# One program for all eight batch elements in place of a loop of four passes over two

## The reference

```
x, cond, ctx                     # (8,256,128), (8,128), (8,1601,96)
for each of 12 sublayers s:
    h = layernorm(x) * a_s(cond) + b_s(cond)
    s = 0, 1, 6, 7:   16 heads of 64 (wide): softmax(q k' / 8) v @ wo     # 0, 6 self; 1, 7 cross; 0, 1 with rotary turns
    s = 3, 4, 9, 10:  16 heads of 8 (narrow), 3, 9 self; 4, 10 cross (9 normalises h by head)
    s = 2, 5, 8, 11:  FFN 128 -> 512 -> 128 (8 and 11 gated)
    x = x + (gate_s(cond) *) result                                      # gates in 9, 10, 11
```

## Time and profile before

| | |
|---|---|
| median of 3 runs | 7247.16 us (7244.05 to 7248.84) |
| profiled execution | 7236.4 us, its span 7234.6 us |
| TensorE busy | 6467.9 us (89%), 43,254 matmuls |
| VectorE, ScalarE, GpSimd busy | 4933.3 (68%), 3985.1 (55%), 2705.2 us (37%) |
| mean granted clock of TensorE | 0.953 of full speed |
| DMA | 206 MB, mean 28 GB/s |

### The profile page before, as it was taken

One profiled execution on the slowest core, in us unless ns is written; L12 is line 12 of the kernel. 1 busy time (PEld: TensorE's weight loads), 2 busy tenths in 40 slices (PEclk: granted clock), 3 DMA queues, 4 the chain that ended last, 5 costly groups with the idle time before them and its releaser, 6 DMA issues.

```text
span 7234.6 us, 145186 instructions
## 1 busy us (share of the span) xinstructions
PE 6467.9 (89%) x43254; PEld 3723.7 (51%) x43254; DVE 4933.3 (68%) x9902; ACT 3985.1 (55%) x7106; POOL 2705.2 (37%) x2326
## 2 busy tenths in 40 slices
PE   7899989989789998998978999899897999989988
PEld 4555445644455544564445554456444555446644
DVE  6777666656677766665677776666567776766656
ACT  4455665646444566565644455655564445565556
POOL 2446115640145511564014551156401455115640
PEclk9999999999899999999989999999998999999999
DMA  3110011110111001110011110111001111011100
GB/s 80 32 26 25 23 30 28 29 29 12 45 30 30 24 21 31 30 29 26 12 46 30 30 27 19 31 28 30 26 12 46 28 27 27 19 31 28 29 19 12
DMA packets 347835, 205.96 MB, mean 28 GB/s; under 512 B 165005, under 2 KB 319981, under 8 KB 346926
## 3 DMA queue, kind: packets, MB, share of 16 engines
q1 hardware_dynamic: 347054, 196.34, 10.5%
HBM read 105.18 MB, written 1.05 MB: 15 GB/s over the span
## 4 chain that ended last, share of the span: by engine, by line
PE 65%; issue 13%; DVE 9%; ACT 8%; POOL 2%; SPq 1%; DVEq 0%; ACTq 0%; DMA 0%; POOLq 0%
PE ring L1309 32%; PE o_acc L1309 18%; PE scores L1309 14%; DVE max_part L2048 4%; ACT qop L1597 3%; ACT probs L1722 2%; POOL weight_sum L1270 1%; ACT region L1597 1%; DVE o_inv L2079 1%; DVE ring L2024 1%; ACT qm L1597 1%; DVE ring L2027 1%; DVE qop L2007 1%; PE ring L1407 1%; DVE region L2010 0%
## 5 line engine op out<-in xcount | busy, mean ns | idle before, releaser
L2048 DVE TENSOR_REDUCE max_part<-ring 128x1 f32<-128x400 f32 (+2 forms) x4608 | 2454.6, 578 | 865.6 <-PE ring L1309 849.8
L1722 ACT ACTIVATE probs<-scores 128x1024 f32<-128x1024 f32 (+1 forms) x2048 | 1915.7, 968 | 1262.8 <-PE scores L1309 895.3
L1270 POOL TENSOR_TENSOR weight_sum<-weight_sum,probs 128x512 f32<-128x512 f32 (+1 forms) x1408 | 1784.3, 1267 | 103.4 <-ACT probs L1722 4.1
L1309 PE MATMUL o_acc<-probs,region 128*32 128x256 f32 (+2 forms) x13312 | 1361.7, 389 | 0.0
L1270 POOL TENSOR_TENSOR weight_sum<-probs 128x512 f32<-128x512 f32 x256 | 324.3, 1267 | 2159.5 <-PE ring L1309 1913.6
L1597 ACT ACTIVATE region<-ring 64x400 f16<-64x400 f32 (+4 forms) x1744 | 814.4, 477 | 524.7 <-PE ring L1309 415.7
L1309 PEld LDWEIGHTS o_acc<-probs,region 128*32 128x32 f32 (+2 forms) x13312 | 590.2, 123 | 533.1 <-issue 323.3
L1597 ACT ACTIVATE qop<-ring 64x256 f16<-64x256 f32 (+1 forms) x1536 | 563.5, 374 | 485.7 <-DVE ring L2027 313.8
L1309 PE MATMUL scores<-qop,region 128*128 128x256 f16 (+1 forms) x3328 | 779.1, 275 | 18.0 <-ACT probs L1722 9.7
L1309 PE MATMUL ring<-nk,qm 128*128 128x400 f16 (+2 forms) x2560 | 718.1, 343 | 78.2 <-DVE max_part L2048 42.8
L1309 PE MATMUL scores<-qop,x_cop 128*128 128x256 f16 (+1 forms) x3328 | 775.6, 274 | 0.0
(11 more groups left out here) (160 smaller groups left out, 7583.4 us busy)
## 6 DMA issues: line engine op xcount, KB each, us to landing
x_cop<-region SPq DMA_DIRECT2D x256, 200.1 KB, 3.1
stage<-in_wide SPq DMA_DIRECT2D x512, 64.0 KB, 2.0
nk<-region SPq DMA_DIRECT2D x192, 100.1 KB, 2.2
stage<-in_wide SPq DMA_DIRECT2D x128, 128.0 KB, 2.5
v_stage<-in_wide SPq DMA_DIRECT2D x256, 64.0 KB, 1.9
wo_stage<-in_wide SPq DMA_DIRECT2D x32, 512.0 KB, 3.8
cop_few<-kop_few SPq DMA_DIRECT2D x256, 32.0 KB, 1.9
ff_w<-in_ff_w SPq DMA_DIRECT2D x24, 256.0 KB, 4.0
```

The costliest lines, as they stand in the source:

```text
L1270: pool.tensor_tensor(total, before, probs[0:rows_, g % PROBS, at:at + BANK], ALU.add)\
L1309: return pe.matmul(out, lhs, rhs, start=start, stop=stop, skip_group_check=True)
L1722: act.activation(to, src, ACT.Exp, scale=t.scale).then_inc(exp_done.sem, 1)
L2048: dve.tensor_reduce(dst, src, AX.X, ALU.max).then_inc(*release(one))
```

## The change

All four passes are one program and one plan. `make_units` runs over the pairs b, so `u` goes from 0 to 7, there are 384 units, and `Plan` orders all of them together. `sequence()` lists the preludes: (END, u - 2) stands directly ahead of (0, u). Buffers are indexed by `u % 2`, as before by u. `Count.at` returns a constant; `ago`, the credits for the first pass and the pass-end padding of the ring's counts go. The `ab` tile goes: instructions read the table `mod_flat[:, u]`. The result's store has a semaphore for each of two buffers, and VectorE waits for it two elements later; SP's wait at a pass's end goes. What is computed is the same, instruction by instruction, but for the `ab` copies.

```diff
+    for b in range(B // 2):
+        for t in ATTS:
+            for u in (2 * b, 2 * b + 1):
+                for p in range(t.units):
+                    out.append(Unit(len(out), t, u, p, chunk, wide_at, narrow_at))
...
+def sequence():
+
+    out = []
+    for b in range(B // 2):
+        for t in ATTS:
+            for u in (2 * b, 2 * b + 1):
+                if t.sub == 0 and b:
+                    out.append((END, u - 2))
+                out.append((t.sub, u))
+    return out + [(END, B - 2), (END, B - 1)]
...
@@ make_order @@
         if un.p == 0:
+            if t.sub == 0 and un.u >= 2:
+                place_prelude(END, un.u - 2, host)
             place_prelude(t.sub, un.u, host)
...
@@ Plan.pre @@
-            on("DVE", 0.4)
+
+            on("DVE", 0.4, *([("SP", ("pre", 1, u - u % 2 - 1, of_kind(1, "ctx")[-1]))] if u >= 2 else []))
...
+            sent = [("SP", ("pre", END, u - 2, m))] if s == END and u >= 2 else []
+            on("DVE", 1.3 if s == END else 0.45, pe, *sent)
...
@@ Count @@
-    def at(self, b, key, c=0):
-        return b * self.total + (self.base[key] + c + self.credit)
+    def at(self, key, c=0):
+        return self.base[key] + c + self.credit
...
@@ SP @@
-                wait((x_out_sent.sem, x_out_sent.at(b, (END, 1), 16)))
-                sp.sem_inc(x_out_free.sem, 2)
...
-            with sp.Fori(0, B // 2 - 1) as b:
-                one_pass(b, True)
-            one_pass(B // 2 - 1, False)
+            program()
...
@@ tensor, the same on the other engines @@
-            with pe.Fori(0, B // 2) as b:
-                program(b)
+            program()
...
@@ make_scores @@
-                    old, co, ago = chunk_before(g, SLOTS)
-                    pe.wait_ge(exp_done.sem, (exp_done.ago if ago else exp_done.at)(b, old.n, co + 1))
+                    if g >= SLOTS:
+                        old, co = chunk_before(g, SLOTS)
+                        pe.wait_ge(exp_done.sem, exp_done.at(old.n, co + 1))
...
@@ modulate @@
-                    dve.wait_ge(ab_ready.sem, ab_ready.at(b, (0, 0), 1))
-                    dve.tensor_scalar(h_t[:, u, :], ring[:, bank(one), 0:N], ab[:, u, 2 * sub:2 * sub + 1],
-                                      ab[:, u, 2 * sub + 1:2 * sub + 2], ALU.mult, ALU.add).then_inc(*release(one))
+                    dve.tensor_scalar(h_t[:, u % 2, :], ring[:, bank(one), 0:N], mod_flat[:, u, 2 * sub:2 * sub + 1],
+                                      mod_flat[:, u, 2 * sub + 1:2 * sub + 2], ALU.mult, ALU.add).then_inc(*release(one))
```

## The result

The changed kernel takes 7128.3 us (median of 4 runs, 7116.94 to 7131.75) against 7245.6 before (median of 4, the three of the table above and one more): ratio 0.9837, interval 0.982 to 0.9854, so 117 us less. Run again beside the experiments it stood at ratios of 0.9829 and 0.9838. The prediction was 7095, with 7000 to 7190 as its range.

The account below looks back on a forecast made before the run. The prediction took TensorE, busy 89%, as the bound wherever it has no holes. Boundaries 60 plus register steps 90 made 150 us off the profiled 7236.4, giving 7086; adjusted to the runs' median, about 7097, written 7095, range 7000 to 7190.

Parts of the forecast that it names:

- (1): Where batch pairs meet: weaving one pair's end with the next's begin saves 20 us per boundary, 60 in all (13 to 86).
- The idle-time working: At the boundary: TensorE's 41.2 us idle falls to 20.6, plus 4 from a faster clock, 25 us saved in all.
- the twin: Sublayer 4's second batch followed by sublayer 6's first, already woven inside a pass: 157.2 us, the model for the boundary.
- The other working: At the boundary: 157.2 us plus 26.0 for rotary work gives 183.2 instead of 200.6, saving 17.4 us.
- (2): Waits on TensorE, VectorE and ScalarE: removing register arithmetic ahead of them saves 90 us (0 to 258).
- TensorE's 25: TensorE's own register steps, beside its matmuls: removing them saves 25 us, lower bound nothing, 113 at 0.01 us a step.
- Rival A: Register steps on all engines are hidden, so only the boundaries pay: 7187 us; chance 0.17.
- (3): Job order moved in the first sublayer and sublayer 6 of pairs 1 to 3: costs nothing, -12 to +12 us.
- (4): Small things: the `ab` copy, its waits, the pass-end store wait and four sem_incs; costed at nothing.
- B: At the boundary, the woven end delays sublayer 0's VectorE jobs, so only the branch is saved: 7144 us; chance 0.11.
- D: At the boundary, the weave keeps the pair of stages at clock 0.67, making the kernel slower: 7275 us; chance 0.03.
- C: Boundaries and register steps both at their upper ends, 86 + 145 + 40: 6976 us; chance 0.06.

Follow-up runs that it names:

- e5: The changed kernel itself, run again unedited beside other experiments: 7113.5 us, ratio 0.9829 to the kernel before.
- e12: The changed kernel itself, run once more unedited beside other experiments: 7119.9 us, ratio 0.9838 to the kernel before.
- e1: Against the kernel before: one pair's plan written out four times in the old order, no loop, branch, register steps or weave; 7217.9 us against 7238.8, ratio 0.9968.
- e2: The changed kernel with a register step put back ahead of each wait on TensorE, VectorE and ScalarE: 7145.5 us, ratio 0.9871 to the kernel before.
- e10: The changed kernel with register steps put back ahead of the waits of VectorE and ScalarE alone: 7141.8 us, ratio 0.9866 to the kernel before.
- e9: The changed kernel with register steps put back ahead of TensorE's waits alone: 7114.3 us, ratio 0.9828 to the kernel before.
- e11: The changed kernel with TensorE's wait for a free ring bank written twice: 7140.7 us, ratio 0.9868 to the kernel before.
- e4: The changed kernel without waits its engine already made for that semaphore with the same or a higher number: 7097.3 us, ratio 0.9803 to the kernel before.

## Why the prediction was right in sum, and where its steps were not

**The sum.** 150 us were forecast, 117 came; the sign and the range held. But terms were wrong by more than the sum was, in opposite senses: that they cancelled to within 33 us is luck.

**(1) The boundary: 60 forecast, 86 to 89 found.** By the stage rows it is 29.0, 30.0 and 29.8 us for the three boundaries, a little over the upper bound of 28.8 that the sum had; some 4.3 us of each are the branch. In e5 and e12 the three come to 89 and 86. The step that failed is "I take 20, between the two workings", with the 4 us for the clock in it. The idle-time working was exact: the twin's 20.6 us of idle time was to be the woven pair's, and the pair has 20.4. What was too small is the clock: I let only the 13.9 us of the end's own matmuls speed up, but the low level had lain over others of the pair too. It lasted 34 us of the 200.6 and now 10 of the 171.6, and the pair's work went from 159.4 to 151.2, 8 us in place of 4. The other working, by the twin's length, added 26 us for rotary work, the difference of two second batches; of the first batches in the changed kernel it is 20 (75.2 against 55.0 for sublayer 6 of pair 0). The check "near 183, and not 195" came out at 171.6.

**(2) The register steps: 90 forecast, some 10 to 30 found.** e1 leaves about 9 us beside the branch, in the old order; e2 puts 24 to 30 on putting them back into the new one. Pair 0, which was to isolate this term, reaches the end of its last stage but one, with the order still that of before, at 1723.7, 1720.6 and 1713.5 us in the changed kernel's three executions, against 1721.1 before: a gain of 2 us on the mean, where 90 us over four pairs would have been about 22. The price of a hop with one step, 0.08 us, was right (78 ns). The step that failed is the share on the path: "I take 65, under the middle" from a chain of waits whose shares for DVEq and ACTq rounded to nothing. e10 says 22. The other half, TensorE's 25, had no row of its own; by e9 it comes to nothing, because its place was taken by a cost that the prediction named only as a smaller gain: "where two waits stay, a wait instruction takes one step's place". On TensorE that instruction costs 0.09 us more in the hop than the step did, and 4,072 more of them cost 21 us (e11). That the "issue" share fell from 13% to 4% of the chain with so little time saved shows how little a share of the last chain says of what a removal brings. Rival A was nearer in size for this term, though the steps are not hidden, only mostly off the path; the time it gave, 7187, was too high because it kept (1) at 60 and (3) at nothing. Of the rule in the Trainium skill (Advanced Engine Details and Errata, Sequencer Loop), that further instructions are read and queued while a control instruction executes, the trace shows both: on TensorE the step did not hold up the matmul (47 ns with it), on ScalarE it did (101 against 23 ns).

**(3) The table's numbers: nothing forecast, about 26 found.** The failed step is "TensorE waits there for VectorE's chain, not for the moved jobs". It did wait for VectorE, but for the bank that VectorE was to free, and the moved jobs decide which bank is asked for and when. The bounds, 12 us to either side, were taken from a stage's repeats in one order and could say nothing of another order.

**(4)** The small things were nothing, as costed; the page has 9.6 MB in the two queues for instructions before and 7.7 now, so the program written out fetches no more than the loop did. The rivals: B (the end delays sublayer 0) fell with the 20.4 us of idle time; D (clock held at 0.67) came out the other way, the clock rose from 0.91 to 0.97, as the Trainium skill (TensorE: Matmul & The Clock Gate, Part 1) would have it of denser work. C's 6976 took 40 us for TensorE's steps, which is not the upper end of 113 that (2) had stated; at the upper ends it would have been 6903.

Together, by the stages of the two profiled executions, which are 107 us apart: the three boundaries are 88.8 us shorter, the four sublayers 6 are 39.6 shorter (about 24 of it by the order), the four second batches of sublayer 3 are 14.7 longer, by the clock alone as e5 and e12 show, and all other stages together are 6.7 longer. In e5 and e12 these four are 89.0 and 85.9 shorter, 34.2 and 35.1 shorter, 6.9 and 2.9 longer, and 7.4 and 3.6 shorter. Outside the boundaries and sublayer 6 the register steps thus brought nothing that stands clear of the clock.

## What to carry to other kernels

Where two loop turns meet and the busiest engine has little to do, weave them, and count both the idle time of the nearest twin and what the clock gives back on all work of the stretch, not only on the part that moved. Price a hop and its share on the path apart: the hop can be right and the term several times too large. When a list schedule (a plan that places each job at the first time its inputs and engine allow) is run anew over a longer program, compare its order stage by stage, since a job that moves past a bank's release can be worth as much as a term that was costed with care. Before a stage's length is laid to an edit, compare its idle time and its clock with a second execution of the same program.

## What was not expected of the hardware

A register step on ScalarE behind a release costs 78 ns in the hop (101 against 23 ns, and 174 with two of them). On TensorE it costs none in the hop (47 ns with it, and 47 in e4, where a lone wait sits on the instruction); a separate wait instruction on TensorE costs 89 ns (136 against 47), so constants in the place of registers lengthened some of its hops. One program's executions differ by 4.0 us in a stage of 38.5 us with the idle time equal, by the granted clock alone.
